# Six input transposes, the first expert's two weight splits and four first-layer blocks of a mixture, moved in among the last steps of the attention ahead of it

## The chip, the cores and the metric

The kernel runs on one core of a Trainium2 chip. The metric is the device time of one execution in microseconds (us). The engines are named as in the profile: PE is TensorE's matmul, PEld its weight load, DVE VectorE, ACT ScalarE, POOL GpSimd and SP the engine that issues the transfers.

## The reference

Six layers run one after the other on x of 16 sequences, 128 positions and 256 channels, each followed by a residual and a layer norm. The change concerns the first two:

```python
scores = jnp.einsum('bqhe,bkhe->bhqk', Q, K) / np.sqrt(d_head)   # 16 heads of 64, causal mask
A = jax.nn.softmax(scores, axis=-1)
z = jnp.einsum('bhqk,bkhe->bqhe', A, V)
attn_out = jnp.einsum('bqhe,hed->bqd', z, W_O) + b_O
...
h = jax.nn.relu(jnp.einsum('edi,bsi->bsed', proj_in, x))         # 8 experts, 512 hidden units
o = jnp.einsum('eid,bsed->bsei', proj_out, h)
gate = jnp.einsum('bks,bkse->bse', weights, onehot)
return jnp.einsum('bsei,bse->bsi', o, gate)
...
x = _layernorm(x + _L0_attn_ref(x, ...), axis=-1)
x = _layernorm(x + _L0_xattn_ref(x, ctx_512, itok_BxS2xS_0_7, ...), axis=-1)
```

The later four layers (a routed feed-forward, two attentions with narrow heads, a second mixture) are not touched.

## The kernel before

Every product that needs full precision is made of three matmuls (`split3`, L83 to L85): each operand is kept as a high part and a low part, and high by high, low by high and high by low are added up in PSUM. So each input of a product is split first: ACT copies the high part out of PSUM, DVE subtracts it from the PSUM value and writes the low part. Weights arrive by transfer in one of two `raw` buffers, and `split_unit` (L603, L605) makes the two parts from there on DVE.

**The first attention** (functions whose names begin with `w_`) works on pairs p = 0 to 31: a pair is one sequence b = p // 2 and half of its heads. Four pairs are a group G of two sequences. The order on each engine is written out by hand as a loop over steps p = 0 to 36. On PE a step holds the scores of pair p (L344, L350), the transposes of the probabilities of pair p - 2 (L361), at even steps the output product of sequence (p - 4) / 2 (`out_project`, 24 matmuls), and the values product of pair p - 2 (L374, `values`). Up to step 27, projections of the next group (`w_of_step`) stand in between. In steps 28 to 36 there is no next group and these places are empty. On ACT a step copies the high part of z of pair p - 3 (`z_hi`, L436), a transposed half (L431), four exponentials (L424), the other transposed half and four more exponentials. On DVE a step holds the two row maxima of pair p (L487), the reciprocals of pair p - 1, the low part of z of pair p - 3 (`z_lo`, L497), some gates of the mixture (L506), and at odd steps the norm of sequence (p - 5) / 2 (`norm_a`, `norm_b`, the latter ending with L524). POOL multiplies the probabilities by the reciprocals (L276).

**The first mixture** (`M2`, functions whose names begin with `mix_`) runs 8 experts. Its steps have letters in `mix_order`: ("x", k) transposes one of the two 128-channel chunks of four sequences (k = 0 to 7; PE L655, ACT L736, DVE L811); ("u", u) is one block of the first layer, 128 hidden units for 512 positions (six matmuls of 512 columns into PSUM bank u % 2; ACT L731 and DVE L827 split the result); ("d", u) is the block's second layer, 12 matmuls of 256 columns; ("w", k) is the split of one half of the first expert's weights. They are called x0 to x7, u0, u1 and so on, d0, and the weight halves below. Before the change the start is `[("w", 0)] + x0..x3 + [("w", 1)] + [u0, x4, x5, u1, x6, x7]`, then `u2, d0, u3, d1, u4, d2` and so on, and TensorE begins with

```python
w_tensor(pe)
pe.wait_ge(stage_done, 1)
mix_tensor(pe, M2, mix_tensor_parts(pe, M2))
```

where `stage_done` is raised by DVE when the last layer norm of the attention is done. The same signal lets POOL build a selector for the third layer (`ffn_selector_pool`, L1010 and L1014). The second mixture (`M6`) already starts inside the attention ahead of it; that is not changed.

Of the kernel before, what the change touches and what calls it, by code (L numbers as in the profile page):

```python
# [19 lines left out]
P = 128  # L20
B, S, D = 16, 128, 256
DC = D // P
GB = 4
# [64 lines left out]
def program(nc, x_in, ctxT_in, itokT_in, w_a1, w_e1i, w_e1o, w_ffn, w_a4, w_a5, w_e6i, w_e6o,  # L88
# [118 lines left out]
    m = r2.again()  # L207
    W.XT = pair(m, "wXT", [P, DC, WT])
    W.QT = m.place("wQT", [P, 2, 8, WT], F32)
    W.KT = m.place("wKT", [P, 2, 8, WT], F32)  # L210
    W.V = m.place("wV", [P, 2, GW, H, 64], F32)
# [4 lines left out]
    W.r = m.place("wr", [P, 2, D], F32)  # L216
# [65 lines left out]
    def w_tensor(pe):  # L282
# [50 lines left out]
        def scores(p):  # L333
# [13 lines left out]
            for i in range(QH):  # L347
                for half in range(2):
                    rows64 = slice(64 * half, 64 * half + 64)
                    last = nc.tensor.matmul(ps[:, WSB[half], i * S:(i + 1) * S], W.QT[rows64, G % 2, 4 * u + i, tok],  # L350
                                            W.KT[rows64, G % 2, 4 * u + i, tok], start=False, stop=i == QH - 1)
                    if i == QH - 1:
                        last.then_inc(s["s_full"], 1)
# [10 lines left out]
        def values(p):  # L364
# [7 lines left out]
            for i in range(QH):  # L372
                for half in range(2):
                    last = nc.tensor.matmul(ps[64 * half:64 * half + 64, WZB, i * S:(i + 1) * S],  # L374
                                            W.V[:, G % 2, b % GW, 8 * u + 2 * i + half, :], W.PT[:, half, i, :],
# [17 lines left out]
        for p in range(NP + 5):  # L393
# [14 lines left out]
            for kind, i in f[3:]:  # L408
                fill(kind, i)

    def w_scalar(act):
# [29 lines left out]
        for p in range(NP + 5):  # L441
# [7 lines left out]
            for kind, (G, j) in w_of_step(p):  # L449
                if kind == "x":  # L450
                    x_hi(G)

# [4 lines left out]
    def w_vector(v, link, extra):  # L457
        s = W.s

        def fill(kind, i):  # L460
# [7 lines left out]
            else:  # L468
                v.wait_ge(s["g_full"], F + 1)
                two = bank.rearrange("p (c t) -> p c t", c=2)  # L470
                if kind == "q":
                    last = nc.vector.scalar_tensor_tensor(W.QT[:, G % 2, 2 * j:2 * j + 2, :], two, 1 / 8.0,
                                                          W.bq8[:, 2 * j:2 * j + 2].unsqueeze(2).broadcast_to([P, 2, WT]),
                                                          ALU.mult, ALU.add)
                elif kind == "k":
                    last = nc.vector.tensor_tensor(W.KT[:, G % 2, 2 * j:2 * j + 2, :], two,
                                                   col_bk1[:, 2 * j:2 * j + 2].unsqueeze(2).broadcast_to([P, 2, WT]), ALU.add)
                else:
                    b, half = divmod(j, 2)
                    last = nc.vector.tensor_tensor(W.V[:, G % 2, b, half * 8:(half + 1) * 8, :],  # L480
# [50 lines left out]
        for p in range(NP + 5):  # L531
# [20 lines left out]
            for kind, i in f[3:]:  # L552
                fill(kind, i)
        for b in range(B):
# [9 lines left out]
    def mix_setup(tag, gelu, win, wout, first, pair0, per):  # L564
# [4 lines left out]
        c.XT = pair(m, tag + "XT", [P, DC, B * S])  # L569
        if gelu:  # L570
            m.at = n_km_at
        c.hT = pair(m, tag + "hT", [P, HC, GT])
        if gelu:
            c.slots = slots6
# [6 lines left out]
        else:  # L581
            c.slots = [pair(m, f"{tag}w{i}", [P, 2 * RAW]) for i in range(2)]
        c.end = m.at
# [1407 lines left out]
```

## Time and profile before

| | |
|---|---|
| time, median of 3 runs | 1692.24 us (1685.35 to 1699.0) |
| the profiled execution's own time | 1693.69 us |
| its span, first to last instruction | 1691.9 us |
| PE busy, share of the span | 1599.5 us, 95% |
| DVE, ACT, POOL busy | 60%, 40%, 11% |
| mean granted clock of TensorE | 0.962 of full speed |

Busy shares are means over the whole span. Times of single stretches below are microseconds from the start of the span; the attention's last steps and the mixture's first ones lie between 290 and 360.

### The profile page before, as it was taken

Reading aid. Unit: us, or ns where it says so; the run is one execution under the profiler, and the core shown is the slowest. Engines: PE = TensorE matmul, PEld = TensorE weight load, DVE = VectorE, ACT = ScalarE, POOL = GpSimd, SP = SyncE. Lnnn points to the kernel's source line nnn. Section 1 sums busy time; section 2 is a strip of 40 time slices with the busy share of each in tenths; the row PEclk is TensorE's granted clock in tenths of the full one; section 3 lists DMA queues with packets and bytes.
Section 4 is the critical chain, followed back from the end, with each engine's and each line's share of the span. In section 5 each row is a group of like instructions: output and inputs, shape, how many; then the busy total and the mean of one; then the engine's idle time right before and its main releaser. Section 6 shows DMA issues by size and latency. Waiting matters only on the chain.

```text
span 1691.9 us, 28465 instructions
## 1 busy us (share of the span) xinstructions
PE 1599.5 (95%) x11048; PEld 1435.1 (85%) x11048; DVE 1012.5 (60%) x2176; ACT 677.7 (40%) x1777; POOL 181.5 (11%) x174
## 2 busy tenths in 40 slices
PE   6999999799999999899998699999998899999997
PEld 5888888689898989788887599999998798989896
DVE  6776777564545445766655466667774554444446
ACT  1554454422222222123332366656664344444443
POOL 1222232210000000020000231111110000000001
PEclk9999999989999999989999799989988799999999
DMA  5000100011011101000001855667660000000001
GB/s 200 2 14 1 39 2 1 1 61 38 24 38 36 37 24 37 19 20 13 31 1 15 114 70 68 81 74 115 80 88 14 13 26 26 25 26 12 25 12 50
DMA packets 43064, 66.50 MB, mean 39 GB/s; under 512 B 4560, under 2 KB 33488, under 8 KB 42832
## 3 DMA queue, kind: packets, MB, share of 16 engines
q1 hardware_dynamic: 42960, 65.09, 19.7%
q8 instruction: 68, 1.11, 0.3%
q14 instruction: 36, 0.29, 0.1%
HBM read 36.24 MB, written 2.10 MB: 23 GB/s over the span
## 4 chain that ended last, share of the span: by engine, by line
PE 85%; DVE 8%; issue 2%; ACT 2%; DMA 1%; SPq 1%; POOL 0%; DVEq 0%; POOLq 0%; ACTq 0%
PE ps L83 22%; PE ps L84 21%; PE ps L85 21%; PE ps L1538 6%; PE ps L1525 3%; PE ps L350 2%; PE ps L374 2%; PE ps L1515 2%; PE ps L361 2%; PE ps L344 1%; PE ps L1512 1%; DVE X L863 1%; DVE negm L1716 1%; DMA nQs<-nQc_h 1%; SPq L1373 1%
## 5 line engine op out<-in xcount | busy, mean ns | idle before, releaser
L825 DVE TENSOR_TENSOR m6hT_l<-m6h,m6hT_h 128x512 fp32r<-128x512 f32 x128 | 88.4, 692 | 188.1 <-ACT m6hT_h L729 188.0
L731 ACT ACTIVATE m2hT_h<-ps 128x512 fp32r<-128x512 f32 x128 | 76.7, 599 | 282.1 <-PE ps L85 282.1
L827 DVE SCALAR_TENSOR_TENSOR m2hT_l<-ps,m2hT_h 128x512 fp32r<-128x512 f32 x128 | 88.5, 691 | 157.4 <-ACT m2hT_h L731 157.4
L728 ACT ACTIVATE m6h<-ps,m6b 128x512 f32<-128x512 f32 x128 | 88.3, 690 | 218.8 <-PE ps L85 204.2
L1624 ACT ACTIVATE nPr<-ps,negm 128x128 f32<-128x128 f32 x512 | 146.2, 371 | 67.3 <-DVE negm L1716 67.0
L1716 DVE TENSOR_REDUCE negm<-ps 128x4 f32<-128x512 f32 x128 | 88.1, 688 | 101.4 <-PE ps L1515 101.2
L83 PE MATMUL ps<-w_h,m6hT_h 128*128 128x256 f32 x512 | 145.0, 283 | 2.6 <-DVE X L863 2.0
L85 PE MATMUL ps<-w_h,m6hT_l 128*128 128x256 f32 x512 | 145.8, 285 | 0.0
L1538 PEld LDWEIGHTS ps<-nV,nPT 128*128 128x128 f32 x1024 | 130.9, 200 | 16.9 <-issue 14.9
L84 PE MATMUL ps<-w_l,m6hT_h 128*128 128x256 f32 x512 | 145.1, 283 | 0.0
L85 PE MATMUL ps<-m2w_h,m2hT_l 128*128 128x256 f32 x512 | 144.9, 283 | 0.0
L84 PE MATMUL ps<-m2w_l,m2hT_h 128*128 128x256 f32 x512 | 144.8, 283 | 0.0
L83 PE MATMUL ps<-m2w_h,m2hT_h 128*128 128x256 f32 x512 | 144.3, 282 | 0.0
L1538 PE MATMUL ps<-nV,nPT 128*128 128x17 f32 x1024 | 131.0, 261 | 12.2 <-DVE nz L1681 8.2
L83 PE MATMUL ps<-m6XT_h,w_h 128*128 128x512 f32 x256 | 104.3, 407 | 8.2 <-DVE m6hT_l L825 8.2
L83 PEld LDWEIGHTS ps<-w_h,m6hT_h 128*128 128x128 f32 x512 | 98.2, 192 | 8.5 <-issue 2.7
L85 PE MATMUL ps<-m6XT_h,w_l 128*128 128x512 f32 x256 | 102.8, 402 | 0.0
L84 PE MATMUL ps<-m6XT_l,w_h 128*128 128x512 f32 x256 | 102.8, 401 | 0.0
L83 PE MATMUL ps<-m2XT_h,m2w_h 128*128 128x512 f32 x256 | 102.3, 400 | 0.3 <-DVE m2hT_l L827 0.2
L84 PEld LDWEIGHTS ps<-w_l,m6hT_h 128*128 128x128 f32 x512 | 98.0, 191 | 5.4
L83 PEld LDWEIGHTS ps<-m2w_h,m2hT_h 128*128 128x128 f32 x512 | 97.8, 191 | 5.4
L84 PEld LDWEIGHTS ps<-m2w_l,m2hT_h 128*128 128x128 f32 x512 | 97.8, 191 | 4.7
(270 smaller groups left out, 4297.5 us busy)
## 6 DMA issues: line engine op xcount, KB each, us to landing
nKm<-nKc_h SPq DMA_DIRECT2D x64, 128.0 KB, 4.6
nQs<-nQc_h SPq DMA_DIRECT2D x64, 128.0 KB, 6.6
raw<-in_w_e1i SPq DMA_DIRECT2D x9, 512.0 KB, 3.2
raw<-in_w_e1o SPq DMA_DIRECT2D x9, 512.0 KB, 3.2
raw<-in_w_e6i SPq DMA_DIRECT2D x9, 512.0 KB, 3.4
raw<-in_w_e6o SPq DMA_DIRECT2D x9, 512.0 KB, 3.3
raw<-in_w_a SPq DMA_DIRECT2D x8, 512.0 KB, 4.5
nKm<-nKc_l SPq DMA_DIRECT2D x32, 128.0 KB, 5.3
```

Source lines behind the costliest of these rows:

```text
L83: nc.tensor.matmul(out, wh, xh, start=start, stop=False, **kw)
L84: nc.tensor.matmul(out, wh, xl, start=False, stop=False, **kw)
L85: return nc.tensor.matmul(out, wl, xh, start=False, stop=stop, **kw)
L350: last = nc.tensor.matmul(ps[:, WSB[half], i * S:(i + 1) * S], W.QT[rows64, G % 2, 4 * u + i, tok], W.KT[rows64, G % 2, 4 * u + i, tok], s ...
L728: nc.scalar.activation(c.h32[:, u % 2, :], ps[:, u % 2, :], ACT.Gelu, bias=bias)
L731: nc.scalar.activation(c.hT[0][:, ch, :], ps[:, u % 2, :], ACT.Relu).then_inc(c.s["hi_ready"], 1)
L825: last = nc.vector.tensor_tensor(c.hT[1][:, ch, :], c.h32[:, u % 2, :], c.hT[0][:, ch, :].bitcast(F32), ALU.subtract)
L827: last = nc.vector.scalar_tensor_tensor(c.hT[1][:, ch, :], ps[:, u % 2, :], 0.0, c.hT[0][:, ch, :].bitcast(F32), ALU.max, ALU.subtract)
L1525: last = nc.tensor.transpose(ps[:, TB[n % 2], i * S:(i + 1) * S], N.Pr[:, n % 4, i, :], ident[:, :])
L1538: last = nc.tensor.matmul(ps[:, ZB5, h * ZW:(h + 1) * ZW], N.PT[:, n % 2, i, :], N.V[:, G % 2, b, h, :], start=True, stop=True)
L1624: last = nc.scalar.activation(N.Pr[:, i % 4, j, :], ps[:, SB[i % 2], j * S:(j + 1) * S], ACT.Exp, bias=negm[:, i % 4, j:j + 1])
L1716: nc.vector.reduce_max(negm[:, i % 4, :], ps[:, SB[i % 2], :].rearrange("p (h k) -> p h k", h=QH), AX.X, negate=True).then_inc(s["s_max"], 1)
```

## The change

The first mixture's start is interleaved with steps 28 to 35 of the attention. A new table gives the places: the two weight halves are split at steps 28 and 30, x0 to x5 follow steps 28 to 33, and u0 to u3 follow steps 32 to 35, each behind all of that step's own work, on every engine that takes part. What is left behind the attention is d0, d1, u4, x6, x7, d2, u5 and so on. TensorE no longer waits for `stage_done`; x0, x2, x4 and x6 wait for the norms of their own four sequences, x0 also for the last projection of the attention, and u0 and u1 for the last exponentials, because they write the PSUM banks of the scores. The SBUF layout is rearranged so that the mixture's tiles lie on buffers that the attention has finished with: Q, K and V are two tiles each, by the parity of the group, and the first expert's weights have a slot of their own in the region of the attention's weights.

```diff
+    W_X_AT, W_U_AT, W_W_AT = 28, NP, (28, 30)
+
+    def w_following(p):
+
+        return ([("w", W_W_AT.index(p))] if p in W_W_AT else []) + \
+            ([("x", p - W_X_AT)] if 0 <= p - W_X_AT < M_EARLY_X else []) + ([("u", p - W_U_AT)] if 0 <= p - W_U_AT < M_EARLY else [])
...
@@ w_tensor, end of step p (w_scalar likewise)
+            for kind, i in w_following(p):
+                if kind == "x":
+                    after["x"](i)
+                elif kind == "u":
+                    after["u"](0, i)
...
@@ w_vector, end of step p
+            for kind, i in w_following(p):
+                if kind == "w":
+                    split_unit(v, c2.first, i, cut(c2.slot0, i * RAW, RAW), RAW)
+                elif kind == "x":
+                    mix_transposed_x(v, c2, i)
+                else:
+                    after["u"](0, i)
+                    after["w"](0, i)
...
@@ mix_order
-        if c.gelu:
-            start = [("d", 0), ("d", 1)]
-        else:
-            start = [("w", 0)] + [("x", k) for k in range(4)] + [("w", 1)]
-            start += [("u", 0), ("x", 4), ("x", 5), ("u", 1), ("x", 6), ("x", 7)]
+        start = [("d", 0), ("d", 1)]
...
-        for u in range(M_EARLY if c.gelu else 2, NU + 2):
+        for u in range(M_EARLY, NU + 2):
             start += [("u", u)] if u < NU else []
-            if c.gelu and u == M_EARLY:
+            if u == M_EARLY:
                 start += [("x", 6), ("x", 7)]
...
@@ transposed_x and up, on TensorE
-            if c.gelu and ch == 0:
-                pe.wait_ge(N.s["x_done"], (NG + g + 1) * GB)
+            if ch == 0:
+                pe.wait_ge(*((N.s["x_done"], (NG + g + 1) * GB) if c.gelu else (W.s["x_done"], (g + 1) * GB)))
+            if k == 0 and not c.gelu:
+                pe.wait_ge(W.s["g_evac"], w_fill(NGW - 1, "v", 3) + 1)
...
+            if first and u < 2 and not c.gelu:
+                pe.wait_ge(W.s["p_exp"], 2 * NP - 1 + u)
...
@@ the engines' programs
-            w_tensor(pe)
-            pe.wait_ge(stage_done, 1)
-            mix_tensor(pe, M2, mix_tensor_parts(pe, M2))
+            m2 = mix_tensor_parts(pe, M2)
+            w_tensor(pe, m2)
+            mix_tensor(pe, M2, m2)
```

The first place is TensorE at steps 32 and 33. Before, the values product of pair 30 (L374), the transposes of pair 31 (L361), the values product of pair 31 and the output product of sequence 15 follow each other directly; wzT is z, wA the attention's weights:

```order
L374 MATMUL ps<-wPT,wV 64x128 x8
L361 MATMUL ps<-ident,wPr 128x128 x8
L374 MATMUL ps<-wPT,wV 64x128 x8
L83 MATMUL ps<-wA_h,wzT_h 128x256
L84 MATMUL ps<-wA_l,wzT_h 128x256
L85 MATMUL ps<-wA_h,wzT_l 128x256
```

After (L390, L377 and L686 are the old L374, L361 and L655; m2w_117 and m2w_118 are the first expert's weights, high and low):

```order
L390 MATMUL ps<-wPT,wV_99 64x128 x8
L686 MATMUL ps<-ident,X 128x128 x4
L83 MATMUL ps<-m2XT_h,m2w_117 128x512
L84 MATMUL ps<-m2XT_l,m2w_117 128x512
L85 MATMUL ps<-m2XT_h,m2w_118 128x512
...
L377 MATMUL ps<-ident,wPr 128x128 x8
L390 MATMUL ps<-wPT,wV_99 64x128 x8
L686 MATMUL ps<-ident,X 128x128 x4
```

Now x4 and the six matmuls of u0 stand between the values product of pair 30 and the transposes of pair 31, and x5 (and u1 behind it) between the values product of pair 31 and the last output product.

The second place is VectorE at steps 31 to 34. Before, from the norm of sequence 13 (L524) on:

```order
L524 TENSOR_SCALAR X<-wr,mv,rstd 128x256
L492 RECIPROCAL wrec<-wsums 128x8
L497 TENSOR_TENSOR wzT_l<-ps,wzT_h 128x512 x2
L514 TENSOR_TENSOR wr<-ps,wXB 128x256
```

After (L550, L518, L523 and L540 are the old L524, L492, L497 and L514; L845 is x's low part, L861 u's):

```order
L550 TENSOR_SCALAR X<-wr,mv,rstd 128x256
L845 TENSOR_TENSOR m2XT_l<-ps,m2XT_h 128x512
L518 RECIPROCAL wrec<-wsums 128x8
L523 TENSOR_TENSOR wzT_l<-ps,wzT_h 128x512
L845 TENSOR_TENSOR m2XT_l<-ps,m2XT_h 128x512
L861 SCALAR_TENSOR_TENSOR m2hT_l<-ps,m2hT_h 128x512
L523 TENSOR_TENSOR wzT_l<-ps,wzT_h 128x512
L540 TENSOR_TENSOR wr<-ps,wXB 128x256
```

The low part of x3 stands ahead of `z_lo` of pair 29, and those of x4 and u0 ahead of `z_lo` of pair 30.

## Rows read from the trace of the kernel before

**Rows 1.** The page, chain of work that ended last, by engine
```profile
PE 85%; DVE 8%; issue 2%; ACT 2%; DMA 1%; SPq 1%; POOL 0%; DVEq 0%; POOLq 0%; ACTq 0%
```

**Rows 2.** Windows: length, busy PE, PEld, DVE, ACT, POOL; clock, DMA share, GB/s
```profile
291.96:337.09 45.13, 34.69 (x314) 28.71 (x312) 26.06 (x73) 21.64 (x83) 13.33 (x14) 0.92 0.00 1
337.09:358.95 21.86, 16.92 (x86) 14.78 (x87) 15.75 (x23) 6.85 (x12) 4.87 (x4) 0.77 0.15 49
```

**Rows 3.** The same view, shorter windows, for the granted clock
```profile
300.00:310.00 10.00, 7.82 (x68) 5.61 (x66) 6.82 (x19) 5.42 (x21) 2.63 (x3) 0.83 0.00 1
...
325.00:330.00 5.00, 5.00 (x38) 4.60 (x38) 0.00 (x0) 0.41 (x1) 0.40 (x1) 0.66 0.00 0
...
337.00:345.00 8.00, 3.06 (x14) 2.60 (x14) 6.03 (x9) 1.20 (x2) 4.87 (x4) 0.63 0.07 12
345.00:350.00 5.00, 5.00 (x21) 4.26 (x20) 3.90 (x5) 2.41 (x5) 0.00 (x0) 0.57 0.23 89
```

**Rows 4.** Timeline of PE, last attention steps: start, duration, instruction, [wait before <- releaser]
```profile
304.65 1.77 PE L374 MATMUL ps<-wPT,wV 128*64 128x128 f32 x16 [2.14 <-ACT wPT L431]
...
323.89 0.39 PE L83 MATMUL ps<-wA_h,wzT_h 128*128 128x256 f32 x1 [1.84 <-DVE wzT_l L497]
...
331.30 1.09 PE L374 MATMUL ps<-wPT,wV 128*64 128x128 f32 x16 [0.74 <-ACT wPT L431]
333.95 0.39 PE L83 MATMUL ps<-wA_h,wzT_h 128*128 128x256 f32 x1 [1.55 <-DVE wzT_l L497]
```

**Rows 5.** Timeline of PE behind the attention
```profile
339.91 1.94 PE L655 MATMUL ps<-ident,X 128*128 128x128 f32 x8 [2.82 <-DVEq L803]
343.97 1.97 PE L655 MATMUL ps<-ident,X 128*128 128x128 f32 x8 [2.12 <-DVE m2XT_l L811]
...
351.05 1.03 PE L655 MATMUL ps<-ident,X 128*128 128x128 f32 x8
351.84 0.48 PE L83 MATMUL ps<-m2XT_h,m2w_h 128*128 128x512 f32 x1
...
356.13 0.28 PE L83 MATMUL ps<-m2w_h,m2hT_h 128*128 128x256 f32 x1
...
357.56 0.40 PE L83 MATMUL ps<-m2XT_h,m2w_h 128*128 128x512 f32 x1
...
358.95 0.28 PE L83 MATMUL ps<-m2w_h,m2hT_h 128*128 128x256 f32 x1
```

**Rows 6.** Timeline of DVE over both
```profile
301.58 1.29 DVE L487 TENSOR_REDUCE negm<-ps 128x4 f32<-128x512 f32 x2 [2.53 <-PE ps L350]
...
308.97 1.29 DVE L487 TENSOR_REDUCE negm<-ps 128x4 f32<-128x512 f32 x2 [1.08 <-PE ps L350]
...
316.87 1.29 DVE L487 TENSOR_REDUCE negm<-ps 128x4 f32<-128x512 f32 x2 [3.52 <-PE ps L350]
...
323.20 0.64 DVE L497 TENSOR_TENSOR wzT_l<-ps,wzT_h 128x512 fp32r<-128x512 f32 x1
...
340.05 1.18 DVE L603 TENSOR_SCALAR m2w_h<-raw 128x1024 fp32r<-128x1024 f32 x1 [0.44 <-DVE X L524]
...
343.23 1.28 DVE L811 TENSOR_TENSOR m2XT_l<-ps,m2XT_h 128x512 fp32r<-128x512 f32 x2
...
347.21 0.68 DVE L603 TENSOR_SCALAR m2w_h<-raw 128x1024 fp32r<-128x1024 f32 x1
...
349.16 0.69 DVE L827 SCALAR_TENSOR_TENSOR m2hT_l<-ps,m2hT_h 128x512 fp32r<-128x512 f32 x1
```

**Rows 7.** Timeline of ACT
```profile
330.17 1.08 ACT L431 ACTIVATE wPT<-ps 128x512 f32<-128x512 f32 x2
...
348.53 0.60 ACT L731 ACTIVATE m2hT_h<-ps 128x512 fp32r<-128x512 f32 x1 [1.96 <-PE ps L85]
```

**Rows 8.** Timeline of POOL
```profile
303.06 2.08 POOL L276 TENSOR_TENSOR wPr<-wPr,wrec 128x512 f32<-128x512 f32 x2 [4.51 <-DVE wrec L492]
...
340.82 3.51 POOL L1014 TENSOR_SCALAR_AFFINE_SELECT f3sel<-f3sel 128x1024 f32<-128x1024 f32 x2
```

More of the change, by code:

```diff
@@ L349, in scores @@
                     rows64 = slice(64 * half, 64 * half + 64)
-                    last = nc.tensor.matmul(ps[:, WSB[half], i * S:(i + 1) * S], W.QT[rows64, G % 2, 4 * u + i, tok],
-                                            W.KT[rows64, G % 2, 4 * u + i, tok], start=False, stop=i == QH - 1)
+                    last = nc.tensor.matmul(ps[:, WSB[half], i * S:(i + 1) * S], W.QT[G % 2][rows64, 4 * u + i, tok],
+                                            W.KT[G % 2][rows64, 4 * u + i, tok], start=False, stop=i == QH - 1)
                     if i == QH - 1:
@@ L451, in w_scalar @@
                     x_hi(G)
+            for kind, i in w_following(p):
+                if kind == "x":
+                    after["x"](i)
+                elif kind == "u":
+                    after["u"](0, i)
     def w_vector_start(v):
@@ L475, in fill @@
                 elif kind == "k":
-                    last = nc.vector.tensor_tensor(W.KT[:, G % 2, 2 * j:2 * j + 2, :], two,
+                    last = nc.vector.tensor_tensor(W.KT[G % 2][:, 2 * j:2 * j + 2, :], two,
                                                    col_bk1[:, 2 * j:2 * j + 2].unsqueeze(2).broadcast_to([P, 2, WT]), ALU.add)
@@ L479, in fill @@
                     b, half = divmod(j, 2)
-                    last = nc.vector.tensor_tensor(W.V[:, G % 2, b, half * 8:(half + 1) * 8, :],
+                    last = nc.vector.tensor_tensor(W.V[G % 2][:, b, half * 8:(half + 1) * 8, :],
                                                    bank.rearrange("p (h e) -> p h e", h=8),
@@ L553, in w_vector @@
                 fill(kind, i)
+            for kind, i in w_following(p):
+                if kind == "w":
[3 more added lines that the diff above has]
+                else:
+                    after["u"](0, i)
+                    after["w"](0, i)
         for b in range(B):
@@ L582, in mix_setup @@
             c.slots = [pair(m, f"{tag}w{i}", [P, 2 * RAW]) for i in range(2)]
+            c.slot0 = [Region(nc, r1.start + at * KB, 8 * KB).place(f"{tag}w{at}", [P, 2 * RAW], F32R) for at in (8, 40)]
         c.end = m.at
@@ L677, in up @@
                 pe.wait_ge(prep_done, i * c.per + (c.pair0 + 2 * e2))
-            wh, wl = (t[:, 0:RAW].rearrange("p (k n) -> p k n", k=DC) for t in c.slots[e2])
+            slot = c.slot0 if first and e2 == 0 else c.slots[e2]
+            wh, wl = (t[:, 0:RAW].rearrange("p (k n) -> p k n", k=DC) for t in slot)
             pe.wait_ge(c.s["lo_ready"], i * NU + u + 1)
@@ L693, in down @@
                 pe.wait_ge(c.s["comb_done"], i * (2 * B) + GB * (q + 1))
-            wh, wl = (t[:, RAW:2 * RAW].rearrange("p (k n) -> p k n", k=HC) for t in c.slots[e2])
+            slot = c.slot0 if type(i) is int and e2 == 0 else c.slots[e2]
+            wh, wl = (t[:, RAW:2 * RAW].rearrange("p (k n) -> p k n", k=HC) for t in slot)
             for j in range(GB):
```

58 lines of the change are left out of this document (32 added, 26 removed).

## The prediction

> **What bounds the kernel now.** I read the chain of waits first: 85% of it is TensorE [rows 1]. The kernel is as long as PE's work, plus the places where PE stands idle, plus the places where its clock is granted at the lower level. So a change of order can only win idle time and low-clock time. The second view is the table of windows around the border. From 291.96, where step 28 begins, to 337.09, where the last output product ends, PE is busy 34.69 of 45.13 us, so it is idle 10.44 us [rows 2]. From there to 358.95, where d2 starts, it is busy 16.92 of 21.86 us: idle 4.94 us [rows 2]. Third, PE's timeline says what each idle piece waits for. In the attention's steps it is a copy by ACT (2.14 and 0.74 us) or the low part of z on DVE (1.84 and 1.55 us) [rows 4]; there are seven such pieces, and these are four of them. Behind the attention it is the last layer norm (2.82 us) and then DVE, which splits weights ahead of the transposes' low parts (2.12 us) [rows 5]. Fourth, the clock: it is 0.83 in the mean of 300 to 310, 0.66 in 325 to 330, and 0.63 and 0.57 in the two windows from 337 to 350 [rows 3]. The levels are 2.4 and 1.2 GHz, so a mean of 0.83 over 10 us means some 3.4 us at the lower level, and 0.66 over 5 us means 3.4 us too. In the same way the last two windows hold 5.9 and 4.3 us. Each of the first two dips costs about 1.7 us of PE's work, half of its length.
>
> **Prices of the moved blocks at the full clock.** Two transposed chunks take 351.84 - 351.05 = 0.79 us, one therefore 0.40. A first-layer block takes 358.95 - 357.56 = 1.39 us, a second-layer block 357.56 - 356.13 = 1.43 us [rows 5]. On DVE the low part of one chunk takes 1.28 / 2 = 0.64 us, that of a block 0.69 us, and one weight half 349.16 - 347.21 = 1.95 us when undisturbed [rows 6]. On ACT a high part takes 0.60 us [rows 7].
>
> **What the change removes behind the attention.** Of the 21.86 us, the work is 4 x 0.79 + 5 x 1.39 + 2 x 1.43 = 12.97 us at the full clock. Idle time is 4.94 us and the lower clock therefore 16.92 - 12.97 = 3.95 us. In the changed order only d0, d1, u4, x6 and x7 stand between the attention's last product and d2: 2.86 + 1.39 + 0.79 = 5.04 us. I see no wait in it. d0 to d2 need only low parts that are made earlier. x6 needs the last norm, which before was done 2.8 us after the last product. It will be done later now, because DVE has the low part of u2 ahead of that norm: u2 ends 1.39 us behind the product, its two parts take 0.60 + 0.69 us, and the norm takes about 2.5 us more, together some 5.2 us. PE reaches x6 only after u2, u3, d0, d1 and u4, 2.78 + 2.86 + 1.39 = 7.0 us, so that is covered by 1.8 us. So the stretch shrinks by 21.86 - 5.04 = 16.82 us. This is the gross gain.
>
> **What it adds to the attention's steps, in order.** PE runs its instructions in program order, and the new blocks stand at the end of a step, not in the idle places. Those idle places are waits for a chain that starts with the step's own scores (maximum on DVE, exponentials and copies on ACT). So a block at a step's end does not fill the wait; it delays the next scores and all that hangs on them.
>
> - x0 to x3: 4 x 0.40 = 1.6 us, all on the path.
> - DVE's part of steps 28 to 30. Behind step 28 come the first weight half and x0's low part, 1.95 + 0.64 = 2.59 us, against 2.53 us of idle time ahead of the maxima of step 29 and the 0.40 us by which these come later [rows 6]. It just fits. x1's 0.64 us has 1.08 us of idle time, and the second half with x2 has 3.52 us [rows 6]. I cost all of this at nothing. Without that cover it would cost up to 2 x 1.95 + 3 x 0.64 = 5.8 us.
> - x3's low part stands ahead of `z_lo` of pair 29, which ends the 1.84 us wait of the output product [rows 4, 6]. DVE is the late one there: `z_lo` began at 323.20 right behind other work. So some of the 0.64 us is new delay. PE is already 1.6 us later by x0 to x3 while DVE's chain is only moved by x0 to x2, 1.2 us, so 0.64 - 0.40 = 0.2 us remain.
> - x4 and u0: 0.40 + 1.39 = 1.8 us.
> - The next values product waits for ACT. ACT now has u0's high part and `z_hi` of pair 30 ahead of the two transposed halves: from the end of u0 that is about 0.55 + 0.55 + 1.08 = 2.2 us (copies overlap a little, so 0.55 for each 0.60) [rows 7]. PE has 1.1 us of transposes in that time, so it idles 1.1 us in place of 0.74: 0.3 us more.
> - x5 and u1: 1.8 us.
> - The last output product waits for `z_lo` of pair 31. Behind u1 come u1's high part on ACT, its low part on DVE, then `z_lo`: 0.60 + 0.69 + 0.64 = 1.9 us plus little, in place of 1.55 us [rows 4, 6, 7]: 0.4 us more.
> - u2 and u3 behind it: 2.8 us.
>
> The sum is 1.6 + 0.2 + 1.8 + 0.3 + 1.8 + 0.4 + 2.8 = 8.9 us. Net gain: 16.8 - 8.9 = 7.9 us. In short, the moved work of 7.9 us stays on the path; what is won is the 4.94 us of idle time and 3.95 us of low clock behind the attention, less 0.9 us of new delay.
>
> **Other queues.** SP waits less: its next weight loads hang on the splits and start some 40 us earlier, and before they landed in time. POOL's selector still starts at `stage_done`, which now comes after u3's low part and another weight half, so it runs beside d0 to u5, where DVE has slack. Nothing behind d2 changes in order. The new SBUF places are read and written by the same shapes; I cost them at nothing, and no row speaks for another price.
>
> **Where the skill speaks.** One split beside POOL's selector took 343.23 - 340.05 = 3.18 us in place of 1.95 [rows 6, 8]. The Trainium skill (SBUF — State Buffer, "Who interferes with whom") says that a VectorE operation which uses the port pair it shares with GpSimd and a GpSimd operation exclude each other for the whole instruction; by that rule, the trace agrees, and it speaks against weight splits put in steps where POOL multiplies. If the first split met a multiply here, step 29 would come 1.2 us later less a slack of 0.3, and the gain would be 7.0 us. Against it, POOL has been idle for 4.51 us when it starts its multiply at 303.06 [rows 8], and the split would run from 299 to 301.
>
> **Rivals.**
>
> *The clock stays up.* More work in the tail might keep the full clock in 300 to 310 and 325 to 330. Each dip that goes is 1.7 us: gain 9.6 or 11.3 us, profiled time 1684 or 1682. For it: PE has 8 us more work there. Against it: up to step 31 only 0.40 us is added to each step of 7 to 8 us, and the idle pieces remain. The Trainium skill (TensorE: Matmul & The Clock Gate, "What's actually happening") holds that the throttled state is the default and activity releases it; by that rule this is the rival to take. Chance 0.17.
>
> *Another dip.* The idle pieces at the end grow (1.1 and 1.9 us in place of 0.74 and 1.55), and the clock could fall once more in the last output product or u2, as it did at 325. One more dip like it is 1.7 us: gain 6.2 us. One of 10 us of unbroken work at the lower level is 5 us: gain 3 us. Chance 0.18.
>
> *VectorE has no room.* If the work I cost at nothing (5.8 us) lands on the path, because waits between its parts are longer than the idle time I read, the gain is 2.1 us. For it: the fit behind step 28 is within 0.4 us. Against it: 3.52 us for the second half. Chance 0.09.
>
> *Slower.* With nothing but short pieces of work between waits, the clock might go down at the output product of step 32 and stay at 1.2 GHz until the mixture's unbroken work. An output product takes 3.1 us (333.95 to 337.09), a values product and a pair's transposes 1.1 us each [rows 2, 4]. From there to d2 there are 3.1 + 1.1 + 1.8 + 1.1 + 1.1 + 1.8 + 3.1 + 2.8 + 5.0 = 20.9 us of work at the full clock; at half of it that is 20.9 us more, 1.7 of which are paid before too. 19.2 - 7.9 = 11.3 us slower, profiled 1705. It decides against the change from 8 us more at the lower level on. Against it: before, the clock came back within 3.4 us each time in the same steps [rows 3]. Chance 0.04.
>
> *It doesn't do what it says.* The order of instructions shows the blocks where the text puts them. That leaves 0.02 that a wait I have not seen gives all of it back.
>
> **How the numbers follow.** My forecast, a gain of 7.9 us, has the remaining chance of 0.50. The profiled execution would go from 1693.69 to 1685.8. That execution is 1.5 us above the median of the three runs, 1692.24, so the median would be 1684.3. The gain lies between 3 and 11.3 us in more than 8 of 10 cases. Runs of the same program stand up to 7 us from their median, which is as large as the gain. I take a range of 1675 to 1696. About 1%, 17 us, is what a measurement of this kernel can tell from no change. A gain of 7.9 us is 0.5%, so "the same" is by far the likeliest. Faster by over 1% needs a gain that no case here gives and comes from scatter alone: 0.08. Slower by over 1% is the slow rival and scatter: 0.04.
>
> **What would show it.** In the changed profile d2 should start near 351, its first-layer neighbours u4, x6 and x7 right ahead of it without waits, and PE's waits of 2.82 and 2.12 us should be gone. In steps 29 to 31 PE's waits should be what they were; ahead of the last values product it should be about 1.1, ahead of the last output product about 1.9 us, on ACT and DVE. The window behind the last output product should show a clock near 1. I am wrong if the maxima of step 29 begin with a wait of PE's scores for DVE, if x6 waits for the norm, or if the border shrinks as I say and the total doesn't.

## The result and the profile after

The changed kernel takes 1678.18 us (median of 20 runs, 1668.84 to 1696.71), the kernel before 1688.92 us (median of 20 runs, 1675.6 to 1699.0). The ratio is 0.9946, with a 95% interval of 0.9924 to 0.9968: 9.1 us less, between 5.4 and 12.8. (The medians are 10.7 us apart; the ratio leaves out one run of the changed kernel, 1696.71 us, that fell in the chip's slower state.) The forecast was 7.9 us less. The median itself, 1678.18 us, is 6.1 us below the 1684.3 forecast, in part because the kernel before has a median of 1688.92 us over 20 runs and not the 1692.24 that the forecast started from. The profiled execution of the changed kernel has a span of 1676.6 us, 15.3 us less than the one before. Only 8.6 us of that lie at the border between the two layers, as the windows show. Of the rest, 8.0 us lie behind d2, where nothing changed in order: from the start of d2 to the end it is 1333 us before and 1325 us after, and 1318 to 1331 us in the experiments below (1324 us in kernel 3, which keeps the order of before). The stretch ahead of step 28 is 1.3 us longer.

These are the windows of the changed kernel: from the start of step 28 to the start of u2 behind the last output product, and from there to the start of d2 (columns as in [rows 2]).

```profile
293.25:343.86 50.61, 39.92 (x351) 33.78 (x350) 35.07 (x85) 25.96 (x91) 13.33 (x14) 0.93 0.07 22
343.86:351.66 7.80, 7.80 (x53) 7.00 (x51) 4.63 (x9) 1.79 (x4) 1.58 (x3) 1.00 0.00 0
```

They answer to [rows 2]. The attention's last steps went from 45.13 to 50.61 us, the stretch behind them from 21.86 to 7.80 us, both together from 66.99 to 58.41 us. The second window has no idle time at all (7.80 busy of 7.80) and the clock at 1.00, where before it was idle for 4.94 us and had a clock of 0.77. Shorter windows show the clock, against [rows 3]:

```profile
300.00:310.00 10.00, 7.87 (x90) 6.13 (x89) 9.12 (x24) 6.04 (x22) 2.63 (x3) 1.00 0.18 53
320.00:325.00 5.00, 3.46 (x28) 3.28 (x28) 4.49 (x15) 4.16 (x18) 2.52 (x3) 0.76 0.00 1
325.00:330.00 5.00, 4.35 (x42) 3.77 (x40) 0.98 (x3) 0.89 (x2) 2.04 (x2) 0.90 0.00 0
...
340.00:345.00 5.00, 5.00 (x27) 4.80 (x27) 0.00 (x0) 0.00 (x0) 0.00 (x0) 0.69 0.00 0
```

The dip in 300 to 310 is gone. The one of 325 to 330 came a little earlier, on x3 and the transposes of pair 30, whose longer run the wait behind them took up. And there is a new one in the last output product, from 339 on, which took 4.47 us where 2.97 us is the time at full speed (kernel 5). PE's timeline of the same steps, against [rows 4] and [rows 5]:

```profile
306.41 1.09 PE L390 MATMUL ps<-wPT,wV 128*64 128x128 f32 x16 [2.13 <-ACT wPT L452]
307.44 0.66 PE L686 MATMUL ps<-ident,X 128*128 128x128 f32 x4
...
312.11 0.39 PE L83 MATMUL ps<-wA_h,wzT_h 128*128 128x256 f32 x1 [1.47 <-DVE wzT_l L523]
...
321.54 1.09 PE L390 MATMUL ps<-wPT,wV 128*64 128x128 f32 x16 [2.13 <-ACT wPT L452]
322.56 1.12 PE L686 MATMUL ps<-ident,X 128*128 128x128 f32 x4
323.47 1.92 PE L377 MATMUL ps<-ident,wPr 128*128 128x128 f32 x8
...
326.04 0.39 PE L83 MATMUL ps<-wA_h,wzT_h 128*128 128x256 f32 x1 [0.65 <-DVE wzT_l L523]
...
334.31 1.09 PE L390 MATMUL ps<-wPT,wV 128*64 128x128 f32 x16 [1.28 <-ACT wPT L452]
...
339.39 0.39 PE L83 MATMUL ps<-wA_h,wzT_h 128*128 128x256 f32 x1 [2.01 <-DVE wzT_l L523]
```

The waits of 2.13 us for ACT stand where they stood, with the new transposes behind them, not in them. The last two waits are 1.28 and 2.01 us, forecast as 1.1 and 1.9. The wait ahead of the output product of step 30, which I had costed at no change, went from 1.02 to 1.47 us.

### The profile page after: what moved, and what is told of

Same layout as the page of the kernel before. It is cut to its first block, busy times and chain, and to the rows that moved or that the text cites. A ratio compares the mean times of both kernels' runs of the same rounds, so it can differ in the third digit from the quotient of the medians.

```text
span 1676.6 us, 28469 instructions
## 1 busy us (share of the span) xinstructions
PE 1587.0 (95%) x11048; PEld 1423.7 (85%) x11048; DVE 1012.3 (60%) x2176; ACT 676.1 (40%) x1777; POOL 180.4 (11%) x174
## 4 chain that ended last, share of the span: by engine, by line
PE 85%; DVE 9%; issue 2%; ACT 2%; DMA 1%; SPq 1%; POOL 0%; DVEq 0%; POOLq 0%; ACTq 0%
PE ps L83 22%; PE ps L85 21%; PE ps L84 21%; PE ps L1570 6%; PE ps L1557 3%; PE ps L366 2%; PE ps L390 2%; PE ps L1547 2%; PE ps L377 2%; PE ps L360 1%; PE ps L1544 1%; DVE X L897 1%; SPq L1405 1%; DMA nQs<-nQc_h 1%; DVE negm L1748 1%
## 5 line engine op out<-in xcount | busy, mean ns | idle before, releaser
L861 DVE SCALAR_TENSOR_TENSOR m2hT_l<-ps,m2hT_h 128x512 fp32r<-128x512 f32 x128 | 88.5, 691 | 161.9 <-ACT m2hT_h L766 161.8
L1570 PEld LDWEIGHTS ps<-nV,nPT 128*128 128x128 f32 x1024 | 127.5, 196 | 16.8 <-issue 14.8
L85 PE MATMUL ps<-m2w_h,m2hT_l 128*128 128x256 f32 x448 | 126.8, 283 | 0.0
L84 PE MATMUL ps<-m2w_l,m2hT_h 128*128 128x256 f32 x448 | 126.7, 283 | 0.0
L83 PE MATMUL ps<-m2w_h,m2hT_h 128*128 128x256 f32 x448 | 126.3, 282 | 0.0
L85 PEld LDWEIGHTS ps<-w_h,m6hT_l 128*128 128x128 f32 x512 | 97.1, 190 | 0.0
L445 ACT ACTIVATE wPr<-ps,negm 128x128 f32<-128x128 f32 x256 | 90.8, 384 | 4.8 <-DVE negm L513 4.8
L83 PEld LDWEIGHTS ps<-m2w_h,m2hT_h 128*128 128x128 f32 x448 | 85.5, 191 | 4.7
```

The lines of the kernel that those rows point to most:

```text
L83: nc.tensor.matmul(out, wh, xh, start=start, stop=False, **kw)
L84: nc.tensor.matmul(out, wh, xl, start=False, stop=False, **kw)
L85: return nc.tensor.matmul(out, wl, xh, start=False, stop=stop, **kw)
L445: last = nc.scalar.activation(W.Pr[:, p % 3, half, j, :], ps[:, WSB[half], j * S:(j + 1) * S], ACT.Exp, bias=negm[:, n % 4, j:j + 1], accu ...
L861: last = nc.vector.scalar_tensor_tensor(c.hT[1][:, ch, :], ps[:, u % 2, :], 0.0, c.hT[0][:, ch, :].bitcast(F32), ALU.max, ALU.subtract)
L1570: last = nc.tensor.matmul(ps[:, ZB5, h * ZW:(h + 1) * ZW], N.PT[:, n % 2, i, :], N.V[:, G % 2, b, h, :], start=True, stop=True)
```

## The experiments

All are measured by one number from the trace, the **border**: from the start of the values product of pair 25 to the start of d2. (It begins one values product, 1.02 us, ahead of the windows above, because in some traces the first records of step 28 are missing.) It is 68.01 us in the kernel before and 59.43 us in the changed one. A dip is a stretch of low clock; "at the full clock" below means that the excess of such stretches has been taken off by arithmetic, from rows of the same work at full speed. The time of a whole execution scatters by 10 us and more either way, the border mostly by the dips, some 1.5 us each. Every border is that of one execution.

**1. Without the blocks.** u0 to u3 stay behind the attention, all else as in the change.

```diff
-        start = [("d", 0), ("d", 1)]
+        start = [("d", 0), ("d", 1)] if c.gelu else [("u", 0), ("u", 1), ("u", 2), ("d", 0), ("u", 3), ("d", 1)]
...
-            ([("x", ...)] ...) + ([("u", p - W_U_AT)] if 0 <= p - W_U_AT < M_EARLY else [])
+            ([("x", ...)] ...)
```

> The change with u0 to u3 left behind the attention (weight halves and x0 to x5 stay early). Measure: the border, from the start of pair 28's scores to the start of d2; it is 66.99 us in the kernel before and 58.41 us in the changed one. Theory A (a block at a step's end stays on TensorE's path wherever it stands; the gain is idle and low-clock time behind the attention): the four blocks cost their 5.6 us in either place, the two waits that they made longer (0.5 us each) shrink again, border 57 to 59.5 us, time against the kernel before 7 to 10 us less. Theory B (the blocks are hidden beside the attention's waits): they come out into the open, border 62 to 64 us, 3 to 5 us less than before.

The border is 61.50 us by the present measure, which is 60.5 by the one used in the expectation; the time ratio to the kernel before is 0.9966 (0.993 to 1.0001), which just fails to tell it from no change. The border is nearer to theory A, 1 us above its range, and below the range of theory B. It is 2.07 us more than in the changed kernel, and the rows account for most of it. More: u2 waits 0.67 us for u0's low part, and the clock was low in two stretches (x1 and the scores of step 30 took 3.72 us in place of 2.11, the output product of step 32 4.56 in place of 3.05), together 3.8 us. Less: the last output product was at full speed (2.98 in place of 4.47) and the wait at step 30 shorter (1.01 in place of 1.47), together 1.9 us. At the full clock the border is 58.8 against 57.9 us in the changed kernel, so the four blocks cost nearly the same in either place, as theory A has it. One part of my reasoning fell here. The waits at the last values and output products did not shrink:

```profile
334.70 1.09 PE L390 MATMUL ps<-wPT,wV 128*64 128x128 f32 x16 [1.28 <-ACT wPT L452]
338.39 0.38 PE L83 MATMUL ps<-wA_h,wzT_h 128*128 128x256 f32 x1 [2.01 <-DVE wzT_l L523]
344.95 0.50 PE L83 MATMUL ps<-m2XT_h,m2w 128*128 128x512 f32 x1 [0.67 <-DVE m2hT_l L861]
```

They are 1.28 and 2.01 us, exactly as with the blocks. Whatever stands last in a step on PE, a block or only a transpose, has its high part on ACT and its low part on DVE ahead of the next `z_hi` and `z_lo`, and this chain starts when PE is done with it:

```profile
337.05 0.69 DVE L845 TENSOR_TENSOR m2XT_l<-ps,m2XT_h 128x512 fp32r<-128x512 f32 x1 [0.16 <-ACT m2XT_h L771]
337.66 0.68 DVE L523 TENSOR_TENSOR wzT_l<-ps,wzT_h 128x512 fp32r<-128x512 f32 x1
```

**2. The weight halves alone.** The two splits stay early; x0 to x7 and all blocks stand behind the attention in the order of the kernel before.

```diff
-        return ([("w", ...)] ...) + ([("x", ...)] ...) + ([("u", ...)] ...)
+        return ([("w", W_W_AT.index(p))] if p in W_W_AT else [])
...
+        start = [("x", k) for k in range(4)] + [("u", 0), ("x", 4), ("x", 5), ("u", 1), ("x", 6), ("x", 7), ("u", 2), ("d", 0), ("u", 3), ("d", 1)]
```

> Only the two weight halves are early; all transposes and blocks stand behind the attention, and they no longer wait for all of the norms at once. Theory A: x0 and x1 need no norm of the last sequences, so they start at once; the 2.12 us wait for the splits goes, short waits for the low parts of x (about 1 us) come in its place; border 60 to 63 us. Theory B (the moved transposes and blocks bring the gain, the splits nothing): 65 to 67 us. Theory C (the waits behind the attention are the splits' and the norm's alone, and nothing else in the change matters): 58 to 59 us.

The border is 62.37 us (61.35 by the expectation's measure): theory A, 5.6 us less than before. The time ratio is 0.9985 (0.9955 to 1.0015), which can't tell. Of the 5.6 us, 1.5 us are a dip that fell here in the kernel before and not in this trace: the output product and the values product of step 32 took 4.09 us here and 5.58 us in the kernel before. From the end of the last output product to d2 it is 17.65 us, against 21.86 us before: 4.2 us less. So about half of the border's gain of 8.6 us came with the splits' departure from in front of the transposes and the new waits, but by another route than I had written. (The edit does both at once; no run separates them.) x0 does start at once, yet a wait of 2.64 us follows it:

```profile
336.03 1.03 PE L686 MATMUL ps<-ident,X 128*128 128x128 f32 x8
339.70 1.23 PE L686 MATMUL ps<-ident,X 128*128 128x128 f32 x8 [2.64 <-DVE m2XT_l L845]
```

On DVE the low part of x0 stands behind the last norm (336.23 to 338.70), so PE waits for the norm after all, one chunk pair later.

**3. TensorE kept busy, nothing moved.** The kernel before, with 28 transposes of the identity behind the last output product.

```diff
             w_tensor(pe)
+            for k in range(28):
+                nc.tensor.transpose(ps[:, 4, k % 4 * S:(k % 4 + 1) * S], ident[:, :], ident[:, :])
             pe.wait_ge(stage_done, 1)
```

> The kernel before, with 28 transposes of the identity (2.8 us of TensorE at the full clock, their result unused) put where TensorE waits for the last norm. No work of the kernel moves. Theory A, its clock part (3.95 us of the border is low clock that follows idle time): the clock stays up through the first transposes, border 63 to 65 us, 2 to 4 us less than before. Theory D (the clock there is not a matter of TensorE's idle time): border 67 us, no change.

The border is 67.15 us (66.1 by the expectation's measure), only 0.9 us less than before; the time ratio is 0.9978 (0.9948 to 1.0009). The expectation of 2 to 4 us was wrong. x0 and x1 did run at the full clock (1.04 in place of 1.94 us), but x2's wait for DVE grew by what they won, from 2.12 to 2.95 us, and behind it the clock fell again:

```profile
339.64 1.04 PE L656 MATMUL ps<-ident,X 128*128 128x128 f32 x8
343.63 1.26 PE L656 MATMUL ps<-ident,X 128*128 128x128 f32 x8 [2.95 <-DVE m2XT_l L812]
```

**4. Kept busy in both waits.** The same, and 24 more such transposes ahead of x2's wait.

```diff
+            if k == 2 and not c.gelu:
+                for n in range(24):
+                    nc.tensor.transpose(ps[:, 6, n % 4 * S:(n % 4 + 1) * S], ident[:, :], ident[:, :])
             pe.wait_ge(c.s["g_evac"], k + 1)
```

> The kernel before with 28 transposes of the identity ahead of the wait for the norm and 24 more ahead of x2's wait for the low part of x0 (results unused). The first set alone gave a border of 67.15 us against 68.01, because the clock fell again behind the second wait. If the low clock behind the attention is a matter of TensorE's idle time alone, x2 still starts some 52.9 us behind pair 25's values product (VectorE's splits set that), and the rest to d2 takes 12.3 us at the full clock in place of 14.98: border 65 to 65.6 us. If the clock falls there whatever TensorE does: 67 us.

The border is 66.75 us (one execution). The clock was at full speed throughout, from the first idle piece to d2:

```profile
336.60:343.70 7.10, 6.77 (x62) 6.53 (x62) 5.49 (x9) 1.09 (x2) 4.50 (x4) 1.00 0.00 0
343.70:357.56 13.86, 13.02 (x79) 10.99 (x79) 9.99 (x15) 5.76 (x10) 0.38 (x1) 1.00 0.24 77
```

Yet it gave 1.3 us and not 2.4 to 3. x2 starts 52.89 us behind pair 25's values product, as expected. From there to d2 it took 13.86 us, expected 12.3. Of the difference, 0.83 us is a wait: PE, now fast, waits for DVE at a new place, x6 and x7 for the low part of x4 (the last row), because there the second weight half is still split among the transposes' low parts. The other 0.7 us is PE's own work, busy for 13.02 us of the second window:

```profile
343.70 1.25 PE L659 MATMUL ps<-ident,X 128*128 128x128 f32 x8 [0.33 <-DVE m2XT_l L815]
...
349.43 1.26 PE L659 MATMUL ps<-ident,X 128*128 128x128 f32 x8 [0.83 <-DVE m2XT_l L815]
```

So two things are shown, with one execution each: the low clock follows PE's idle time there (fill the first wait, and the clock stays until the second; fill both, and it stays to d2), and of the 3.95 us of low clock behind the attention some 1.3 us could be had by the clock alone. Ahead of x2 and of x6 DVE was the bound.

**5. More work for VectorE.** The changed kernel with two row maxima (2.3 us together, results unused) ahead of each early split.

```diff
                 if kind == "w":
+                    for n in range(2):
+                        nc.vector.reduce_max(extra_out[:, 2 * i + n:2 * i + n + 1], raw[i % 2][:, :], AX.X)
                     split_unit(v, c2.first, i, cut(c2.slot0, i * RAW, RAW), RAW)
```

> The changed kernel with two row maxima over 1024 columns (about 1.1 us each, results unused) on VectorE ahead of each early weight split, at steps 28 and 30. Measure from here on: the border from the start of pair 25's values product to the start of d2, 68.01 us in the kernel before, 59.43 us in the changed one. Theory A with VectorE's room as the changed trace has it (0.20 us of idle ahead of the maxima of step 29; 1.05 + 0.20 us ahead of those of step 31): 2.2 us more work cost 2.0 us at the first place and 0.9 us at the second, border 62 to 63 us. Rival (VectorE has room beside TensorE's work): border 59 to 60 us.

The border is 61.35 us (one execution), 1.9 us more than the changed kernel's: nearer to theory A than to its rival. PE's waits ahead of the values products of steps 29 and 31 grew from 2.13 us to:

```profile
307.27 1.10 PE L391 MATMUL ps<-wPT,wV 128*64 128x128 f32 x12 [3.57 <-ACT wPT L453]
...
323.99 1.20 PE L391 MATMUL ps<-wPT,wV 128*64 128x128 f32 x16 [2.60 <-ACT wPT L453]
```

That is 1.44 and 0.47 us more, forecast 2.0 and 0.9. A further 0.36 us stands ahead of the output product of step 32, whose `z_lo` begins 4.16 us behind the start of the values product of step 31, 3.80 us in the changed kernel. So the added work costs 2.3 us; a dip in step 30 adds 1.1 us, and the last output product, at full speed here, takes 1.5 us off. Ahead of the two values products, 0.9 and 1.8 us of each 2.3 us added were absorbed, some 0.6 us more than the idle time that I had read (0.20 and 1.25 us). At step 29 the traces show where: the maxima begin 5.04 us behind the start of the values product ahead of them, and 3.24 us in the changed kernel, so 1.8 us of the 2.3 arrive there. The other 0.4 us is on ACT: its exponentials start 0.72 us behind the maxima's start here and 1.09 us in the changed kernel, where they come right behind the copy of a transposed half. The change had left VectorE little room at these steps, but had not gone beyond it at step 28.

**6. Transposes twice, behind the products.** The changed kernel, the transposes of x0 to x3 issued twice.

```diff
+            if not c.gelu and k < 4:
+                for j in range(GB):
+                    nc.tensor.transpose(ps[:, 4 + k % 2, j * S:(j + 1) * S], X[:, g * GB + j, ch * P:(ch + 1) * P], ident[:, :])
```

> The changed kernel with the transposes of x0 to x3 issued twice, at their places behind the values product: 4 x 0.23 to 0.4 us more for TensorE. Theory A: at a step's end they are all on the path, 0.9 to 1.6 us, border 60.3 to 61 us. Theory B (TensorE's waits of 2.13 us absorb them): border 59.4 us. Dips of the clock move by up to 1.5 us from run to run and are taken off by the rows.

The border is 61.65 us (one execution), 2.2 us more than the changed kernel's, above theory A's range because a dip of the clock fell on the values product of step 31 and on x3 (a mean of 0.66 from 320 to 325), 1.3 us. From values product to values product, steps 29 and 31 each went from 6.36 to 6.80 us, so the second sets of x0 and x2, 0.44 us each, are on the path. Step 30 kept its 8.77 us, since there the wait for DVE fell from 1.47 to 1.03 us:

```profile
305.69 1.09 PE L390 MATMUL ps<-wPT,wV 128*64 128x128 f32 x16 [2.13 <-ACT wPT L452]
...
311.38 0.39 PE L83 MATMUL ps<-wA_h,wzT_h 128*128 128x256 f32 x1 [1.03 <-DVE wzT_l L523]
```

So two of the four sets cost what theory A says, that of x1 cost nothing, because DVE was the later of the two there, and that of x3 can't be read beside the dip.

**7. Blocks ahead of the waits.** On PE, x0 to x5 and u0 to u3 ahead of the step's output and values products, behind its transposes. ACT and DVE keep the order of the change.

```diff
@@ w_tensor, step p
+            for kind, i in w_following(p):
+                if kind == "x":
+                    after["x"](i)
+                elif kind == "u":
+                    after["u"](0, i)
             for _, b in w_sequence("o", p, 4):
                 out_project(b)
...
             if 0 <= p - 2 < NP:
                 values(p - 2)
-            for kind, i in w_following(p):
...
```

> The change with the moved transposes and blocks ahead of the step's output and values products on TensorE instead of behind them; ACT and VectorE keep their order. Theory A: now they fill the waits. In the changed kernel TensorE waits 9.7 us in seven places of steps 28 to 34, and 6.6 us of x0 to x5 and u0 to u2 would stand ahead of them; four to six us come off, border 52.5 to 54.5 us, time 12 to 15 us less than before. Theory E (ACT and VectorE are as late as TensorE, and what TensorE wins it waits for at the next place): border 57 to 59 us, as the changed kernel.

The border is 52.06 us, 51.04 by the expectation's measure: 7.4 us less than the changed kernel's, more than expected. The dip in the changed kernel's last output product is 1.5 us of that; at the full clock it is 5.9 us, within the four to six expected. The time is 1673.21 us (median of 6 runs), with a ratio to the kernel before of 0.9897 (0.9854 to 0.994). In the two windows, as above, the clock is at 1.00 in both:

```profile
292.29:336.89 44.60, 38.00 (x354) 32.07 (x355) 35.21 (x86) 26.36 (x92) 13.35 (x14) 1.00 0.08 25
336.89:343.33 6.44, 6.44 (x46) 5.88 (x45) 4.03 (x8) 1.19 (x3) 2.69 (x4) 1.00 0.05 7
```

Step 32 shows how it is won. x4 and u0 stand in the wait for `z_lo`, of which 0.55 us remain:

```profile
319.65 1.09 PE L390 MATMUL ps<-wPT,wV 128*64 128x128 f32 x16 [1.70 <-ACT wPT L452]
320.67 1.09 PE L377 MATMUL ps<-ident,wPr 128*128 128x128 f32 x8
321.60 0.60 PE L686 MATMUL ps<-ident,X 128*128 128x128 f32 x4
321.96 0.48 PE L83 MATMUL ps<-m2XT_h,m2w 128*128 128x512 f32 x1
...
324.14 0.39 PE L83 MATMUL ps<-wA_h,wzT_h 128*128 128x256 f32 x1 [0.55 <-DVE wzT_l L523]
```

From the values product to this output product it is 4.49 us, and 4.50 us in the changed kernel, where nothing but x3 stands there: the 1.8 us of x4 and u0 cost nothing. At steps 33 and 34 no wait is left at all. There the blocks are longer than the waits they fill: values product to values product of step 33 is 3.88 us, against 2.85 us in kernel 2, where nothing stands there at full speed. So x5 and u1, 1.92 us, cost 1.0 us. u2 costs 0.2 us in the same way, and u3, behind the last output product, its 1.39 us. The chain block, high part, low part now runs beside the output and values products.

**8. The transposes alone ahead.** x0 to x5 ahead of the waits, u0 to u3 at the steps' ends.

> Only the transposes x0 to x5 ahead of the waits, the blocks u0 to u3 at the steps' ends as in the change. Theory A: the transposes give what they cost at the step's end, 4 x 0.5 us and a little at x4 and x5, border 56.5 to 57.5 us; the blocks' part of the win (some 5 us: their own 1.4 us three times and the waits of 1.3 and 2.0 us that their high and low parts made) stays away. Rival (the win is the transposes' alone): border 52 to 53 us.

The border is 59.26 us, 2 us above theory A's range and far from its rival's. The time ratio is 0.9913 (0.9886 to 0.9939), which the border does not explain in full. The clock fell in the output products of steps 32 and 34 (4.57 and 4.47 us in place of 3.05 and 2.97), in the changed kernel's trace only in the second. With these excesses taken off on both sides, it is 59.26 - 1.52 - 1.50 = 56.2 against 59.43 - 1.50 = 57.9 us: the transposes give 1.7 us at the full clock, somewhat less than expected (1.9 to 2.9), and the blocks the rest of the way to 52.06. This correction is arithmetic and not a run.

**9. Transposes twice, ahead of the waits.** Kernel 7 with the edit of kernel 6.

> The kernel with the blocks ahead of the waits (border 52.06 us), with the transposes of x0 to x3 issued twice. Theory A: there they stand in a wait that is over 0.5 us long at each of the four places, so the second set costs nothing, border 52.0 to 52.3 us, and each wait behind it is shorter by what was added. Rival: 53 to 53.7 us.

The border is 52.02 us (one execution), against 52.06: nothing, as theory A has it. The waits behind the doubled transposes fell from 1.70 to 1.26 us, by the 0.44 us that kernel 6 paid for in the open, and that of step 30 from 1.16 to 0.72 us:

```profile
304.94 1.09 PE L390 MATMUL ps<-wPT,wV 128*64 128x128 f32 x16 [1.26 <-ACT wPT L452]
...
310.65 0.38 PE L83 MATMUL ps<-wA_h,wzT_h 128*128 128x256 f32 x1 [0.72 <-DVE wzT_l L523]
```

**10. Low parts one step later.** Kernel 7, with the low part of each early x on DVE in the next step, behind `z_lo`.

```diff
                 z_lo(p - 3)
+            for kind, i in w_following(p - 1):
+                if kind == "x":
+                    mix_transposed_x(v, c2, i)
```

> The kernel with the blocks ahead of the waits (border 52.06 us), and on VectorE the low part of each early transposed chunk moved from the end of its step to the next step, behind the maxima, reciprocals and z's low part. Theory A with VectorE's chain as the cause of the waits at the output products of steps 30 and 32: the wait of 1.16 us at step 30 falls by about 0.5 us, and the time from the values product of pair 29 to the output product of sequence 14 falls from 4.49 to about 3.95 us; border 50.9 to 51.3 us, time the same as that kernel's within what can be told. Rival (those waits are ACT's): border 52 us.

The border is 50.97 us, in the range of theory A. From the values product of pair 29 to the output product of sequence 14 it is now 3.98 us, without a wait:

```profile
319.05 1.09 PE L390 MATMUL ps<-wPT,wV 128*64 128x128 f32 x16 [1.70 <-ACT wPT L452]
...
323.03 0.39 PE L83 MATMUL ps<-wA_h,wzT_h 128*128 128x256 f32 x1
```

At step 30 the wait went from 1.16 to 0.62 us. The time is 1671.71 us (median of 6 runs), with a ratio to the kernel before of 0.9892 (0.9853 to 0.9931). It can't be told from kernel 7's by whole runs.

**11. The change again**, in the same rounds as kernel 10.

> The changed kernel itself, on the same chip and in the same rounds as the kernel with the late low parts, for a comparison of the two. Border 58 to 61 us by where the clock dips fall; time 7 to 11 us less than before. The other kernel should be 6 to 10 us faster than this one.

1678.62 us (median of 12 runs), ratio 0.9942 (0.9913 to 0.9971), as in the first measurement. Kernel 10 is 6.9 us faster by the medians of the same rounds. The border of this execution is 61.92 us, 1 us above what I had expected, with dips of the clock in three places (the scores of step 30 took 3.00 us, the output products of steps 32 and 34 4.38 and 4.48 us). In this trace x3 and the transposes of pair 30 ran at full speed, and the wait behind them is 1.94 us in place of 0.65. So 2.5 us of border lie between two executions of one kernel, and all of it is where the clock dips fall. With this trace the border's gain is 6.1 us and not 8.6.

## Why the prediction was right

**The stretch behind the attention** was forecast at 5.04 us and u2 and u3 ahead of it at 2.8 us, together 7.8; it is 7.80 us. No wait appeared, and x6 did not wait for the last norm. This is the step that carried the gain, and it held to the tenth.

**The attention's steps** were forecast to grow by 1.6 + 0.2 + 1.8 + 0.3 + 1.8 + 0.4 = 6.1 us. They grew by 5.5 us, but not by the terms as written. At the full clock they grew by 0.5 us at step 29, 0.9 at step 30, 0.5 at step 31 and 0.5, 2.4 and 2.4 us up to the three products behind it (the values product of pair 30, that of pair 31 and the last output product), together 7.2 us, 1.1 more than forecast. (Each dip is counted with its whole excess.) Measured it is only 5.5 us because the dips took 3.1 us of these steps before and 1.5 us after. The direction was right: the moved work lengthens the steps and fills hardly any wait where it stands (kernels 6 and 9 show both sides, 0.44 us for a doubled chunk in the open and nothing in a wait). The exceptions are step 30, where DVE was late anyway (kernel 6), and x3, which stands ahead of a wait. Of the terms, these were off. x0 to x2 cost 0.50 us and not 0.40 each. Step 30 was costed at nothing for DVE and lost 0.45 us. And x3 cost nothing, since the start of the output product of sequence 14 is set by DVE's chain: 3.96 us behind the values product before, 4.50 in the changed kernel, which is 0.54 for x3's low part where I had 0.2 for it and 0.40 for x3 on PE. x4 with u0, and x5 with u1, take 1.87 us each and not 1.8, and the waits behind them grew by 0.5 us each where I had 0.3 and 0.4.

**The 1.08 us of idle time on DVE at step 30** was misread. It stood there because PE's scores ran at the low clock just then (2.53 in place of 1.62 us). In the changed kernel they ran at full speed, and DVE's maxima follow x1's low part without a gap:

```profile
309.51 0.68 DVE L845 TENSOR_TENSOR m2XT_l<-ps,m2XT_h 128x512 fp32r<-128x512 f32 x1
310.11 1.28 DVE L513 TENSOR_REDUCE negm<-ps 128x4 f32<-128x512 f32 x2
```

Kernel 10 shows what this costs. There x1's low part stands behind these maxima, and step 30, from values product to values product, takes 8.24 us, against 8.78 us in kernel 7. Room on an engine that waits for TensorE has to be read where TensorE's clock is full.

**The fit behind step 28** was right: 2.59 us of work against 2.53 + 0.40, and 0.20 us of idle time were left ahead of the maxima in the changed kernel. The split was not disturbed by POOL either, 300.37 to 302.33.

**The two last waits** had about the right size (1.28 and 2.01 for 1.1 and 1.9), and in the changed kernel they end as forecast, behind the high and low part of u0 and u1. But the blocks are not needed for them: kernel 1 shows the same two waits with only x4 and x5 in front. What costs is any evacuation ahead of `z_hi` and `z_lo`, not a block's.

**The clock.** The forecast left two dips where they were and added none. The changed execution lost the first, kept one that cost nothing in place of the second, and had a new one in the last output product. That is the rivals "the clock stays up" and "another dip" in one. The dips took 1.6 us less than forecast and the terms above 1.1 us more; that is how the border's gain comes to 8.6 us so near the 7.9. This closeness is partly luck: the second trace of the same kernel gives 6.1 us. The sentence that the change wins "4.94 us of idle time and 3.95 us of low clock" is right as a total, but kernels 3 and 4 show that its two parts were not independent. With the clock at full speed and the order as before, PE wins 1.3 us; the rest goes into waits for DVE and into work that is dearer than I had priced it: at full speed the same transposes and blocks kept PE busy for about 14.1 us (1.04 for x0 and x1 in kernel 3, 13.02 from x2 on in kernel 4) and not 12.97, so by these rows the low clock cost nearer 2.9 us than 3.95. What the change removed behind the attention was DVE's chain of norm, split and low parts. In that chain the first weight half took 3.18 us beside POOL's selector where it takes 1.95 us otherwise; the changed kernel's first split, at step 28, takes 1.96 us, so 1.2 us of x2's wait of 2.12 us may be this meeting and not the order alone. No run separates the two.

**VectorE has no room** had a chance of 0.09. It is not what happened, though kernel 5 shows how near it was: 2.3 us more at each of steps 28 and 30, 4.6 in all, cost 2.3 us. The slower rival, a clock that stays low through the tail, appeared in none of the traces of changed kernels.

**The rule of the Trainium skill on the clock** (TensorE: Matmul & The Clock Gate, "What's actually happening": throttled is the default, activity releases it) agrees with kernels 4, 7, 9 and 10. In 4 (behind the attention) and 7 (from step 28 on) the window rows show 1.00 where the same stretch had low clock before. By that rule I might have given the first rival more weight. It did not decide this change, whose blocks leave the waits open, and it did for the placement that fills them.

## What to carry to other kernels

Work moved beside a chain of waits is hidden only where TensorE reaches it before the wait, in program order. At the end of a step whose successor waits for TensorE it lengthens the step by its whole price, and its own evacuation (the copy of its high part and the subtraction for its low part) then stands ahead of the next step's. Ahead of the wait the same blocks cost only what is longer than the wait, and their evacuation runs beside the product behind them (59.43 against 52.06 us of border with the same instructions, 1.5 us of which is a dip). Idle time read on an engine beside a stretch of low clock is partly the clock's, and a low clock beside a wait for another engine is partly that engine's: neither adds up to a gain by itself.

## What the runs showed of the hardware

Where the clock dips fall is not fixed: two executions of the same kernel (the changed one) had one costly dip and three, 59.43 and 61.92 us of border. With the longest wait cut to 1.70 us and those at the end filled, there was none in three traces, from pair 25's values product to d2 (kernels 7, 9 and 10, a mean clock of 1.00 over 52.06, 52.02 and 50.97 us). All ten traces of the kernels that leave the last wait at 1.55 or 2.01 us had at least one between the same two points. These are ten traces against three; what of the waits decides it, their length or their number, no run separates.
